# An audio tower on one core: less arithmetic for offsets, roots and ranks on VectorE, and another order of the pieces

## The reference

```python
# tokens: a deformable convolution, 16 taps a word, 46 words a sequence
off = einsum('bwkc,ock->bow', xr, w_off) + b_off
dy, dx = off[:, 0::2], off[:, 1::2]
px = base + dx                       # base = 16 * word + tap
x0 = floor(px); frac = px - x0
v0, v1 = x at rows x0 and x0 + 1     # zero outside the sequence
wy = max(0, 1 - |dy|)
val = wy * ((1 - frac) * v0 + frac * v1)
h = [cls_token, einsum(val, w_def) + b_def] + positions      # 47 x 128
# attention with an additive estimate
z = layernorm(h)
est = einsum('bqkh,h->bqk', tanh(hq + hk + b1), W2) + b2
h = h + softmax(Q K^T / sqrt(128) + est) V
# eight experts, the best two of a softmax gate, and a shared one
h = h + sum_e combine_e * (relu(z w1_e + b1_e) w2_e + b2_e) + shared(z)
```

## Time and profile before

| | us |
|---|---|
| median of 3 executions | 870.32 (868.21 to 872.73) |
| profiled execution, its own time | 877.52 |
| its span, first to last instruction | 875.7 |
| TensorE busy | 698.9 |
| VectorE busy | 670.8 |
| GpSimd busy | 548.8 |
| ScalarE busy | 515.7 |

### The profile page before, as it was taken

One profiled execution on the slowest core, in us unless ns is written; L12 is line 12 of the kernel. 1 busy time (PEld: TensorE's weight loads), 2 busy tenths in 40 slices (PEclk: granted clock), 3 DMA queues, 4 the chain that ended last, 5 costly groups with the idle time before them and its releaser, 6 DMA issues.

```text
span 875.7 us, 18796 instructions
## 1 busy us (share of the span) xinstructions
PE 698.9 (80%) x6294; PEld 419.6 (48%) x6294; DVE 670.8 (77%) x1750; ACT 515.7 (59%) x903; POOL 548.8 (63%) x588
## 2 busy tenths in 40 slices
...
GB/s 145 208 147 192 93 164 126 130 94 164 76 190 57 197 71 168 104 137 131 129 140 69 191 65 182 79 141 125 122 139 73 112 55 137 50 17 11 25 1 18
...
## 3 DMA queue, kind: packets, MB, share of 16 engines
...
q10 hardware_dynamic: 864, 0.30, 0.1%
...
## 4 chain that ended last, share of the span: by engine, by line
DVE 40%; PE 25%; issue 15%; ACT 7%; POOL 5%; SPq 4%; DMA 3%; DVEq 1%; ACTq 0%; POOLq 0%
POOL G L378 5%; PE bank L936 4%; DVE bank L605 4%; DVE VAL L611 4%; PE bank L959 4%; PE bank L775 3%; DVE G L602 3%; DVE XT L531 3%; PE bank L814 3%; ACT HT L409 3%; DVE GE L724 3%; DVE VT L628 3%; PE bank L850 2%; PE bank L789 2%; DVE TH L650 2%
## 5 line engine op out<-in xcount | busy, mean ns | idle before, releaser
L378 POOL DMA_INDIRECT G<-in_x,idx x576 | 546.5, 949 | 208.5 <-issue 173.4
L409 ACT ACTIVATE HT<-PXB,c_lneg 128x736 f32<-128x736 f32 x192 | 160.1, 897 | 83.3 <-PE bank L814 64.2
L814 PE MATMUL bank<-HT,XN 128*32 128x184 f32 x3072 | 143.5, 335 | 12.8 <-issue 6.7
L936 PE MATMUL bank<-Z,c_w1e 128*128 128x376 f32 x288 | 126.9, 523 | 19.0 <-ACT HE L490 16.9
L416 ACT ACTIVATE HT<-HT 128x2208 f32<-128x2208 f32 x64 | 130.3, 2036 | 0.6
L814 PEld LDWEIGHTS bank<-HT,XN 128*32 128x32 f32 x3072 | 105.7, 115 | 50.1 <-issue 24.2
L775 PE MATMUL bank<-VT,c_wdef 128*128 128x380 f32 x256 | 89.1, 503 | 24.5 <-DVE VT L628 24.5
L959 PE MATMUL bank<-GE,c_w2e 128*128 128x376 f32 x256 | 104.0, 511 | 0.7 <-DVE GE L724 0.7
L531 DVE STREAM_TRANSPOSE XT<-xt 128x768 f32<-128x768 f32 x64 | 59.9, 958 | 52.7 <-DMA xt<-in_x 32.5
L490 ACT ACTIVATE HE<-bank,c_fb 128x376 f32<-128x376 f32 x128 | 73.0, 570 | 40.2 <-PE bank L936 38.6
L724 DVE TENSOR_TENSOR GE<-HE,bank 128x376 f32<-128x376 f32 x128 | 68.8, 538 | 35.2 <-ACT HE L490 25.5
...
## 6 DMA issues: line engine op xcount, KB each, us to landing
xt<-in_x SPq DMA_DIRECT2D x256, 96.0 KB
...
G<-in_x,idx POOLq DMA_INDIRECT x576
...
```

The lines of the kernel that those rows point to most:

```text
L378: pool.indirect_dma_start(out=G[h][:, col, :], out_offset=None, in_=x.rearrange("b (l c) -> (b l) c", c=C), in_offset=bass.IndirectOffsetO ...
L409: act.activation(HT[half][:, c, :, :].rearrange("p g (w n) -> p g w n", n=4), PXB[h][:, :].rearrange("p (g w i n) -> p i g w n", g=NG, i=2 ...
L814: mm = pe.matmul(bank[0][32 * g:32 * g + 32, HW * c:HW * c + HW], XN[h][:, b, C * ch + 32 * c:C * ch + 32 * c + 32], HT[half][:, k, g, :], ...
L936: pe.matmul(cols(2), w1e[:, e, :], Z2[h][:, :], start=True, stop=True).then_inc(up_full, 1)
```

## The change

VectorE's `stage_a` keeps only the positions, the indices and the distance `rest`. The bias of the offsets is added by ScalarE in its copy of them (a3), and a new ScalarE piece a4 (`row_hats`) makes both kinds of hats, with their sign turned, so that `dense_out` multiplies without a factor. The product of row and tap weights is made in c0 in place of the copy to PSUM. `rstd` takes one step of the old kind with other numbers and one of higher order, whose factor 0.375 stands in the matrix `spread` that took the place of `ones`. The maximum of the scores is negated in the reduction. The rank compares once against a table `least` of 0 or the smallest normal number. x of unit 0 is issued by SP and ScalarE, eight transfers each, and the first constants by GpSimd, before its memsets. All four lists of `ORDER` change. A few lines that only rename are left out.

```diff
 ORDER = {
-    "tensor": ("gc n0 fs g0 n1 m0 f0 ds f1 m1 r7 f2 g1 r8 d0 m2 g2 r9 m3 f3 g3 m4 r10 m5 f4 g4 m51 d1 r11 f5 n2 g5 m52 n3 "
-               "r12 d2 f6 g6 d3 b3 f7 g7 a3 d4 a4 d5 d6 d7 d8").split(),
-    "scalar": ("gc k0 fs r6 f0 m0 f1 r7 k1 f2 k2 m3 r9 f3 m41 m4 m5 f4 m51 k3 f5 h0 m52 h1 r12 h2 f6 h3 f7 a3").split(),
-    "vector": ("r6 c0 r7 g0 m1 g1 r8 m2 n0 g2 m3 m4 g3 r10 g4 c1 r11 g5 c2 n1 r12 r13 g6 r14 b3 g7 t0 t1 a4 d8 t2 d9 t3").split(),
-    "sync": ("x0 e0 e1 e2 p0 q0 y0 d9").split(),
+    "tensor": ("n0 fs gc g0 n1 f0 ds m0 f1 m1 r7 d0 g1 f2 r8 m2 g2 f3 m3 r9 g3 m4 d1 r10 m5 f4 m51 d2 g4 f5 m52 r11 g5 n2 "
+               "f6 r12 g6 d3 f7 g7 d4 d5 n3 d6 b3 d7 d8 a3 a4").split(),
+    "scalar": ("gc fs r6 f0 m0 k0 f1 r7 f2 k1 f3 m3 r9 m41 m4 m5 f4 m51 f5 m52 k2 f6 r12 k3 h0 h1 f7 h2 h3 a3 a4").split(),
+    "vector": ("r6 c0 r7 g0 m1 g1 r8 m2 n0 g2 m3 g3 m4 r10 g4 c1 r11 g5 r12 g6 c2 n1 r13 g7 r14 b3 d8 d9 a4 t0 t1 t2 t3").split(),
+    "sync": ("x0 y0 e0 e1 e2 p0 d9 q0").split(),
...
-        offs = sb("offs", [128, NBLK, 8])
-        nw = sb("nw", [128, NBLK, 4])
+        px = sb("px", [128, NBLK, 4])
+        nw = [sb(f"nw{p}", [128, NBLK, 4]) for p in range(2)]
+        rest = sb("rest", [128, GBLK, 4])
         rr = sb("rr", [128, GBLK, 4])
-        e01 = sb("e01", [128, GBLK, 4, 2])
-        e01f = e01[:, :, :, :].rearrange("p t n s -> p (t n s)")
+        e01 = [sb(f"e01{p}", [128, GBLK, 4, 2]) for p in range(2)]
...
+        def load_first(eng, parts):
+
+            for bp in parts:
+                src = x[bass.ds(2 * bp, 2), :].rearrange("b (t w g n) -> g w b t n", t=WG, w=16, g=NG)
+                for g in range(NG):
+                    eng.dma_start(xt[32 * g:32 * g + 32, WG * bp:WG * bp + WG, :], src[g]).then_inc(x_in[bp], 16)
...
-                for r, t in ((0, nw[:, GBLK:NBLK, :]), (1, offs[:, GBLK:NBLK, 4:8])):
+                for r, t in ((1, px[:, GBLK:NBLK, :]), (0, nw[h][:, GBLK:NBLK, :])):
...
-            load_x(0, 0)
+            load_first(sp, (0, 1))
...
+            for name, _s in CONSTS[1:NFIRST]:
+                pool.dma_start(cs[name][:, :], consts[name]).then_inc(first_in, 16)
+            pool.dma_start(ident[:, :], consts["ident"]).then_inc(ident_in, 16)
...
+            pool.memset(spread[:, :], 0.375).then_inc(zeroed, 1)
...
+            load_first(act, (2, 3))
...
-                act.activation(off4[:, :], bank[0][:, 0:XCOLS], ACT.Copy).then_inc(off_ready, 1)
+                act.activation(off4[:, :], bank[0][:, 0:XCOLS], ACT.Identity, bias=cs["boff"][:, 0:1]).then_inc(off_ready, 1)
+
+            def row_hats(m, h):
+                u = 2 * m + h
+                act.wait_ge(ot_read, u + 1)
+                if not (isinstance(m, int) and u < 2):
+                    act.wait_ge(pw_out, 6 * 16 * (u - 1))
+                act.activation(nw[h][:, :, :], offT[:, :, 0:4], ACT.Abs).then_inc(nw_abs, 1)
+                act.wait_ge(nw_abs, u + 1)
+                act.wait_ge(rest_ready, u + 1)
+                act.activation(nw[h][:, :, :], nw[h][:, :, :], ACT.Relu, bias=1.0, scale=-1.0).then_inc(pw_ready, 1)
+                for i in range(2):
+                    act.activation(e01[h][:, :, :, i], rest[:, :, :], ACT.Abs, bias=float(i)).then_inc(e_abs, 1)
+                act.wait_ge(e_abs, 2 * u + 2)
+                e = e01[h][:, :, :, :].rearrange("p t n s -> p (t n s)")
+                act.activation(e, e, ACT.Relu, bias=1.0, scale=-1.0).then_inc(e_ready, 1)
...
+                wait(dve, nw_abs, u)
                 dve.transpose(offT[:, :, :].rearrange("p t r -> p (t r)"), bank[0][:, 0:XCOLS]).then_inc(ot_read, 1)
                 dve.wait_ge(ot_read, u + 1)
                 wait(dve, pw_out, 6 * 16 * u)
-                chain(dve.tensor_tensor(offs[:, :, :], offT[:, :, 0:8], cs["boff"][:, :].unsqueeze(1).broadcast_to([128, NBLK, 8]), ALU.add))
-                chain(dve.tensor_tensor(offs[:, :, 4:8], offs[:, :, 4:8], base, ALU.add))
-                pxg = offs[:, 0:GBLK, 4:8]
+                chain(dve.tensor_tensor(px[:, :, :], offT[:, :, 4:8], base, ALU.add))
+                pxg = px[:, 0:GBLK, :]
                 chain(dve.tensor_scalar(rr[:, :, :], pxg, -0.5, 0.0, ALU.add, ALU.max))
                 chain(dve.tensor_scalar(rr[:, :, :], rr[:, :, :], float(L - 2), ROUND, ALU.min, ALU.add))
                 dve.tensor_tensor(idx[h][:, :].rearrange("p (t n) -> p t n", n=4), rr[:, :, :],
                                   rowb[:, :].unsqueeze(2).broadcast_to([128, GBLK, 4]), ALU.add).then_inc(idx_ready, 1)
+                wait(dve, e_abs, 2 * u)
+                dve.scalar_tensor_tensor(rest[:, :, :], rr[:, :, :], ROUND, pxg, ALU.subtract, ALU.subtract).then_inc(rest_ready, 1)
                 dve.wait_ge(idx_ready, u + 1)
-
-                chain(dve.scalar_tensor_tensor(nw[:, :, :], offs[:, :, 0:4], -1.0, offs[:, :, 0:4], ALU.mult, ALU.max))
-                dve.tensor_scalar(nw[:, :, :], nw[:, :, :], 1.0, 1.0, ALU.min, ALU.subtract).then_inc(pw_ready, 1)
-                dve.wait_ge(pw_ready, u + 1)
-                chain(dve.scalar_tensor_tensor(e01[:, :, :, 0], rr[:, :, :], ROUND, pxg, ALU.subtract, ALU.subtract))
-                chain(dve.tensor_scalar(e01[:, :, :, 1], e01[:, :, :, 0], 1.0, None, ALU.add))
-                chain(dve.scalar_tensor_tensor(e01f, e01f, -1.0, e01f, ALU.mult, ALU.max))
                 chain(dve.tensor_scalar(rowb[:, :], rowb[:, :], float(NB * LP), None, ALU.add))
-                chain(dve.tensor_scalar(e01f, e01f, 1.0, 1.0, ALU.min, ALU.subtract))
-                chain(dve.tensor_tensor(aw[h][:, :, :, :], e01[:, :, :, :],
-                                        nw[:, 0:GBLK, :].unsqueeze(3).broadcast_to([128, GBLK, 4, 2]), ALU.mult))
...
-                    chain(dve.tensor_scalar(ry[:, :].bitcast(i32), ishift[:, :], -1.0, float(0x5F3759DF), ALU.mult, ALU.add))
-                    for _i in range(3):
-                        chain(dve.scalar_tensor_tensor(nt_[:, :], ry[:, :], -0.5, ry[:, :], ALU.mult, ALU.mult))
-                        chain(dve.tensor_tensor(nt_[:, :], nt_[:, :], var[:, :], ALU.mult))
-                        chain(dve.scalar_tensor_tensor(ry[:, :], nt_[:, :], 1.5, ry[:, :], ALU.add, ALU.mult))
+                    chain(dve.tensor_scalar(ry[:, :].bitcast(i32), ishift[:, :], -1.0, float(0x5F1FFFF9), ALU.mult, ALU.add))
+                    chain(dve.scalar_tensor_tensor(nt_[:, :], ry[:, :], -0.703952253, ry[:, :], ALU.mult, ALU.mult))
+                    chain(dve.tensor_tensor(nt_[:, :], nt_[:, :], var[:, :], ALU.mult))
+                    chain(dve.scalar_tensor_tensor(ry[:, :], nt_[:, :], 1.68191391, ry[:, :], ALU.add, ALU.mult))
+                    chain(dve.tensor_tensor(nt_[:, :], ry[:, :], ry[:, :], ALU.mult))
+                    chain(dve.tensor_tensor(nt_[:, :], nt_[:, :], var[:, :], ALU.mult))
+                    chain(dve.scalar_tensor_tensor(nt_[:, :], nt_[:, :], -10.0 / 3.0, nt_[:, :], ALU.add, ALU.mult))
+                    chain(dve.scalar_tensor_tensor(ry[:, :], nt_[:, :], 5.0, ry[:, :], ALU.add, ALU.mult))
...
-                        chain(dve.tensor_copy(awp, aw[h][:, :, :, :].rearrange("p t n s -> p (t n) s")))
+                        dve.wait_ge(e_ready, u + 1)
+                        chain(dve.tensor_tensor(awp.rearrange("p (t n) s -> p t n s", n=4), e01[h][:, :, :, :],
+                                                nw[h][:, 0:GBLK, :].unsqueeze(3).broadcast_to([128, GBLK, 4, 2]), ALU.mult))
...
-                        ins = dve.scalar_tensor_tensor(dst[:, c], got[:, c], -1.0, wy, ALU.mult, ALU.mult)
+                        ins = dve.tensor_tensor(dst[:, c], got[:, c], wy, ALU.mult)
...
-                chain(dve.reduce_max(smx[:, :], SC[:, :, 0:S], AX.X))
-                dve.tensor_scalar(smx[:, :], smx[:, :], -1.0, None, ALU.mult).then_inc(sc_ready, 1)
+                dve.tensor_reduce(smx[:, :], SC[:, :, 0:S], AX.X, ALU.max, negate=True).then_inc(sc_ready, 1)
...
-                eqv = eq[:, :, :, :].rearrange("p t i j -> p t (i j)")
-                chain(dve.scalar_tensor_tensor(eqv, gtv, 0.0, cs["tri"][0:RT, :].unsqueeze(1).broadcast_to([RT, RN, E * E]),
-                                               ALU.is_equal, ALU.mult))
-                chain(dve.scalar_tensor_tensor(gtv, gtv, 0.0, eqv, ALU.is_gt, ALU.add))
+                chain(dve.tensor_tensor(gtv, gtv, least[:, :].unsqueeze(1).broadcast_to([RT, RN, E * E]), ALU.is_ge))
...
+            chain(dve.tensor_scalar(least[:, :], cs["tri"][0:RT, :], -TINY, TINY, ALU.mult, ALU.add))
```

More of the change, by code:

```diff
@@ L38 @@
 ROUND = 8388608.0
+TINY = 2.0 ** -126
 CONSTS = [
     ("ident", [128, 128]), ("wof", [128, KP * 32]), ("selm", [128, 128]), ("base", [128, NBLK * 4]),
-    ("boff", [128, 8]), ("rowbase", [128, GBLK]),
+    ("boff", [128, 1]), ("rowbase", [128, GBLK]),
     ("lneg", [128, CH]), ("wdef", [128, KP * D]), ("bdef", [128, 1]), ("cls", [128, 1]),
@@ L391, in _ @@
             chain = Chain(act, act_chain)
```

(4 more changed lines are left out.)

19 lines of the change are left out of this document (9 added, 10 removed).

## The result

The changed kernel takes 882.22 us (median of 4 executions, 879.71 to 887.07) against 871.53 us of the kernel before on the same chip: ratio 1.0131, 95% interval 1.0066 to 1.0195. It is slower. Its profiled execution took 879.83 us, its span is 877.7 us.

What follows compares the result with a forecast made beforehand. Bound: VectorE's chain with TensorE's answers inside it, GpSimd 2.3 us below. Start -1.6, full steps -3, last steps -2, tail -2.5 gave -9.1 us: 866.6 of 875.7 us profiled, 861 of the median 870.32; eight in ten 838 to 874.

Steps and rivals of the forecast that it cites:

- VectorE's pieces 3.3 us shorter: VectorE, each step: instructions removed from stage_a, roots, ranks and maximum cut its pieces from 44.3 to about 41.0 us.
- ScalarE's five instructions hidden: ScalarE, end of its step: five added small instructions, 1.2 us, hidden behind VectorE's four turns of x (3.6 us).
- The layout of a step: One step laid out: 47.5 us before; after, 32.4 + 15.0 = 47.4 us, taken as 47.0.
- I put 11 full steps at 0.3 us less than before: -3 us: The 11 full steps of the main stretch: each 0.3 us shorter under the new order, -3 us together.
- Steps 12 to 14, -2 us: The three steps without stage_a or turns of x: about 0.6 us gained each, -2 us.
- Start -1.6 us: Kernel start: split loads of x -0.8 us, earlier stage_a of unit 0 -0.8 us; together -1.6 us (-5 to +0.3).
- Tail -2.5 us: Last unit's chain: shorter roots, maximum and ranks, and a shorter step 14; -2.5 us (-1 to -5).
- The queue: SP's list with y0 second: estimate's writes and read back take 11.7 to 12.7 us against 15.0 us, so hidden.
- 1: Rival: layout's waits don't come, GpSimd's gathers bound each step at 45.0 us; 841 us, 834 of the median; 0.22 with halfway.
- 2: Rival: y0's wait on SP delays the softmax 1.5 us a step over 13 steps; +20 us, 881 us; 0.14 with rival 4.
- 3: Rival, no change: step at the layout's 47.4 us or slightly over, start and tail give 3 us; 867 to 870 us; 0.19.
- 4: Rival: hats on ScalarE arrive too late and hold its next step; worth +5 us; 0.14 with rival 2.

Runs made afterwards that it cites:

- x1: The changed kernel with all four old ORDER lists put back, ScalarE's a4 appended last: 851.56 us, 0.9702 of the kernel before.
- x5: The changed kernel with its loop of two steps written out on all engines: 871.56 us, 0.9930 of the kernel before.
- x6: The kernel before with its loop of two steps written out: 865.70 us, ratio 0.9891 to the kernel before as it was.
- x3: The changed kernel with y0 moved from second to last on SP's list: 880.53 us, 1.0105 of the kernel before.

## Why the prediction was wrong

- **VectorE's pieces 3.3 us shorter**: nearly right. Its busy time fell by 42.3 us (46.6 in x1), where I had put about 50, and 207 gaps of 30 to 40 ns, some 7 us, went with it. Of this the whole kernel keeps about half: 3.0% under the old lists and 3.5% under the new ones, 26 to 32 us, where 16 x 3.3 is 53. dense_out at 469 ns (466 before) gains nothing, as I put it.
- **ScalarE's five instructions hidden**: right. They ran from 417.26 to 419.12 us, while VectorE turned x until 422, and VectorE did not wait for them.
- **The layout of a step**: right for the ordinary step in both parts, to 0.3 us, and in most of its waits (above). It gave 47.4 us after; its two parts for before add up to 47.1, not to the 47.5 that the prediction names. So by its own parts there was no gain.
- **"I put 11 full steps at 0.3 us less than before: -3 us"** is the step that failed. I set one ordinary step for all eleven, and took 47.0 where the layout had 47.4. The six ordinary ones among them (3 to 6, 8, 10) did better than that, 1.0 us each by the third combines. But the three steps with a turn of the loop grew by 9.4 us and the first two by 8.3 us. Measured over the eleven: +11.7 us in place of -3. These two kinds of step are what the runs showed in place of the gain. Neither was laid out, though the trace of before shows both (steps of 50 to 51 us, and "issue" in front of TensorE's first products of the turn). At the turn the order puts a long product in front of a short one on which ScalarE's list begins, just where TensorE stands still. x5 and x6 show that the turn is the cause of these long steps (2.0% against 1.1%); that the place of gc is about half of it, one trace on a slow chip shows.
- **Steps 12 to 14, -2 us**: measured +1.1 us over them (-0.7 and +1.9). Step 12 counted from third combine to third combine has its stage_a and its turns, so it was an ordinary one.
- **Start -1.6 us**: unit 1's third combine came 3.9 us earlier, although in the new list it stands behind r12 and g6. But nothing of it was left at the next scores (r6 at 140.6 against 140.4 us). The first gather did not come at 21 us but at 22.5: the transfers of x more than their issue set it, and three turns of x were left to do behind VectorE's last wait. The -0.8 us that I called sure came nearly whole (from TensorE's first product to the first gather 7.6 us in place of 8.4), but behind a start that was 0.6 us later.
- **Tail -2.5 us**: 87.9 us against 94.8, so -6.9; 0.9 of it is the later place of the third combine. Mis-sized, and since the new lists bring most of it (x1's tail, with the old ones, gave -1.1), not for the reasons given.
- **The queue**: y0 hidden by 2 to 3 us was nearly right; there were four waits for the estimate, 0.37 to 3.19 us.
- **The rivals**: 1 did not come in the changed kernel, but in x1's first steps. 2, y0, was refuted by x3, though its 881 us is what the kernel takes (882): had it been my forecast, it would have been luck. 3 was right on the median step. 4 did not come.
- **Added up**: -3.9 at the start, +11.7 in the eleven steps, +1.1 in the last three and -6.9 in the tail are the +2.0 us of the span, against -9.1 forecast. The further 8 us by which the medians differ are in no trace.
- **Still open**: which piece in the head of the list costs the first steps most. ScalarE's k2 and k3 behind m52 are argued from the timeline, not shown by a run that moves them alone. Open too is the part of the lower granted clock.

The version that beats both kernels is x1, the new arithmetic under the old lists: 0.9702.
